# Layer-norm statistics taken in the stage that finishes x, one row tile behind its addition

## The reference, cut to what matters

```python
def _layernorm(x, axis=-1, eps=1e-05):
    m = jnp.mean(x, axis=axis, keepdims=True)
    v = jnp.var(x, axis=axis, keepdims=True)
    return (x - m) / jnp.sqrt(v + eps)
...
    x = x + _L0_gnn_ref(_layernorm(x, axis=-1), edge_index, L0_gnn_weight, L0_gnn_bias)
    x = x + _L0_ffn_ref(_layernorm(x, axis=-1)[None], L0_ffn_Wg, L0_ffn_bg, L0_ffn_We, L0_ffn_be)[0]
```

## Time and profile before

| | |
|---|---|
| time, median of 3 runs | 5624.57 us (5622.45 to 5626.36) |
| the profiled execution's own time | 5618.81 us |
| its span in the profile | 5617.0 us |
| TensorE busy (matmul) | 4898.8 us, 87% |
| TensorE busy (weight load) | 3206.5 us, 57% |
| DVE busy | 2794.0 us, 50% |
| ScalarE busy | 1428.1 us, 25% |
| GpSimd busy | 633.4 us, 11% |

### The profile page before, as it was taken

How to read it: one execution, slowest core, us unless ns; L and a number is a source line. 1 busy time by engine, 2 the same in 40 slices (tenths; PEclk the granted TensorE clock), 3 DMA queues, 4 the chain that set the end, 5 groups by cost and what they waited for, 6 DMA issues and landing times. The chain is left out here.

```text
span 5617.0 us, 281252 instructions
## 1 busy us (share of the span) xinstructions
PE 4898.8 (87%) x116024; PEld 3206.5 (57%) x117274; DVE 2794.0 (50%) x11344; ACT 1428.1 (25%) x4662; POOL 633.4 (11%) x1073
## 2 busy tenths in 40 slices
PE   8899686999898988888888888888888888868789
PEld 6644343444565446666666666666666666644556
DVE  4500344232554665555555555555555555554524
ACT  0000000012232353333333333333333333322313
POOL 0000283000563110000000000000000000010200
PEclk9999897999999999999999999999999999989878
DMA  0000111167443850000000000000000000001000
GB/s 11 15 30 15 28 41 34 45 219 256 137 120 100 296 146 22 12 11 11 11 12 11 11 11 11 12 11 11 11 12 11 11 11 11 8 27 41 16 32 10
DMA packets 153467, 259.51 MB, mean 46 GB/s; under 512 B 47554, under 2 KB 81480, under 8 KB 149037
## 3 DMA queue, kind: packets, MB, share of 16 engines
q1 hardware_dynamic: 98344, 176.13, 9.4%
q0 software_dynamic: 55040, 82.30, 5.1%
HBM read 172.87 MB, written 85.14 MB: 46 GB/s over the span
## 5 line engine op out<-in xcount | busy, mean ns | idle before, releaser
L1558 PE MATMUL bank<-lstm_w,step_h_parts 128*32 128x128 f16 x94848 | 1558.0, 220 | 101.6 <-issue 5.5
L1558 PEld LDWEIGHTS bank<-lstm_w,step_h_parts 128*32 128x32 f16 x94848 | 1341.1, 97 | 451.8 <-issue 300.3
L1630 DVE TRANSPOSE_TENSOR_REDUCE step_summed<-bank 128x4 f32 (+1 forms) x2500 | 792.0, 317 | 1061.1 <-PE bank L1558 895.7
L1553 PE MATMUL bank<-step_xg,step_rows 128*128 (+1 forms) x1252 | 476.0, 381 | 277.9 <-issue 258.2
L1526 ACT ACTIVATE step_act_out<-step_summed,lstm_inv_scale 128x4 f32<-128x4 f32 x625 | 185.8, 297 | 1707.9 <-DVE step_summed L1630 1707.9
L1514 POOL COPY xnT<-step_state 128x4 f32 (+1 forms) x625 | 116.4, 186 | 2743.9 <-DVE step_state L1655 2743.9
L1179 PE MATMUL bank<-sum_parts,sum_hot 125*125 125x512 f16 x1600 | 348.0, 381 | 6.6 <-DVE sum_parts L1138 6.6
L1179 PEld LDWEIGHTS bank<-sum_parts,sum_hot 125*125 125x125 f16 x1600 | 219.8, 137 | 135.2 <-DVE sum_parts L1138 7.7
L1429 PE MATMUL bank<-xg_w,xnT 128*125 128x512 f32 x640 | 277.1, 596 | 6.6 <-DMA xg_w<-in_c_w_ih 6.6
L538 POOL DMA_INDIRECT gcn_rows<-gcn_h_rows,gcn_idx x160 | 202.0, 1262 | 698.6 <-issue 698.3
L1553 PEld LDWEIGHTS bank<-step_xg,step_rows 128*128 128x128 bf16 x2500 | 142.7, 98 | 210.1 <-issue 131.1
(11 more groups left out here) (364 smaller groups left out, 6289.8 us busy)
## 6 DMA issues: line engine op xcount, KB each, us to landing
rel_h<-rel_h_sb SPq DMA_DIRECT2D x39, 1024.0 KB, 6.4
lstm_xg<-cnt POOLq DMA_DIRECT2D x80, 375.0 KB, 4.3
step_xg<-lstm_xg SPq DMA_DIRECT2D x375, 80.0 KB, 2.4
xg_w<-in_c_w_ih SPq DMA_DIRECT2D x16, 1024.0 KB
lstm_w<-in_c_w_hh SPq DMA_DIRECT2D x16, 1024.0 KB, 12.6
cheb_w<-in_L_gnn_weight SPq DMA_DIRECT2D x8, 1024.0 KB
choose_we<-in_L_ffn_experts SPq DMA_DIRECT2D x8, 1024.0 KB
rel_bases<-in_L_gnn_bases SPq DMA_DIRECT2D x8, 1024.0 KB, 11.1
```

Source lines behind the costliest of these rows:

```text
L1553: return nc.tensor.matmul(bank[:], rows[:, p, :], xg[:, at, :], start=True, stop=stop)
L1558: last = nc.tensor.matmul(bank[32 * q:32 * q + 32, 128 * s:128 * s + 128], h_parts[:, c, :], w[:, s, c, q, a, 128 * p:128 * p + 128], star ...
L1630: nc.vector.tensor_reduce(summed[:, 4 * p:4 * p + 4], bank[:, bass.ds(s * 128, 128)].rearrange("p (b r) -> p b r", r=32), X_AXIS, ALU.add, ...
```

## The change: what it does

A semaphore `x_ready` counts finished row tiles of x, five for each layer norm. A new function `take_stats(nc, dve, B, m)` waits for it, takes the `bn_stats` of tile m, and then the `bn_aggr` of tile m - 1. Each stage calls it on DVE: behind the addition of tile m it takes the statistics of tile m - 1, and behind the last addition those of the last tile. For the first layer norm x is the input itself: `x_ready` is raised by five in the constants' block, and edge counting takes the statistics as the first thing on DVE. In `layernorm` only the last tile's `bn_aggr` is left ahead of line 124.

```diff
@@ load_constants
-            nc.vector.memset(B.zero[:], 0.0)
+            nc.vector.memset(B.zero[:], 0.0).then_inc(B.x_ready, NT)
@@ new function
+def take_stats(nc, dve, B, m):
+
+    base = NT * B.ln_calls
+    dve.wait_ge(B.x_ready, base + m + 1)
+    nc.vector.bn_stats(B.stats[:, m, :], B.x[:, m, :]).then_inc(B.ln_stats, 1)
+    if m > 0:
+        dve.wait_ge(B.ln_stats, base + m)
+        nc.vector.bn_aggr(B.mv[:, m - 1, :], B.stats[:, m - 1, :]).then_inc(B.ln_aggr, 1)
@@ layernorm
-            for j in range(NT):
-                nc.vector.bn_stats(B.stats[:, j, :], B.x[:, j, :]).then_inc(B.ln_stats, 1)
-            for j in range(NT):
-                dve.wait_ge(B.ln_stats, base + j + 1)
-                nc.vector.bn_aggr(B.mv[:, j, :], B.stats[:, j, :]).then_inc(B.ln_aggr, 1)
+            dve.wait_ge(B.ln_stats, base + NT)
+            nc.vector.bn_aggr(B.mv[:, NT - 1, :], B.stats[:, NT - 1, :]).then_inc(B.ln_aggr, 1)
             dve.wait_ge(B.ln_aggr, base + NT)
@@ count_edges
         def _(dve):
+            for m in range(NT):
+                take_stats(nc, dve, B, m)
             dve.wait_ge(loaded, 48)
@@ chebyshev
             for m in range(NT):
                 dve.wait_ge(fin, m + 1)
-                nc.vector.tensor_tensor(B.x[:, m, :], B.x[:, m, :], bk[:, 0, m, :], ALU.add).then_inc(fin, 1)
+                nc.vector.tensor_tensor(B.x[:, m, :], B.x[:, m, :], bk[:, 0, m, :], ALU.add).then_inc(B.x_ready, 1)
+                if m > 0:
+                    take_stats(nc, dve, B, m - 1)
+            take_stats(nc, dve, B, NT - 1)
@@ choose_experts
             for e in range(EX):
+                x_step = B.x_ready if e == EX - 1 else added
                 for m in range(NT):
...
-                                                   op0=ALU.mult, op1=ALU.add).then_inc(added, 1)
+                                                   op0=ALU.mult, op1=ALU.add).then_inc(x_step, 1)
+                    if e == EX - 1 and m > 0:
+                        take_stats(nc, dve, B, m - 1)
+            take_stats(nc, dve, B, NT - 1)
@@ add_hidden (LSTM)
                 for c in range(KC):
...
-                    nc.vector.scalar_tensor_tensor(
+                    last = nc.vector.scalar_tensor_tensor(
...
+                last.then_inc(B.x_ready, 1)
+                if m > 0:
+                    take_stats(nc, dve, B, m - 1)
+            take_stats(nc, dve, B, NT - 1)
```

More of the change, by code:

```diff
@@ L62, in allocate @@
     B.bank = [ctx.enter_context(nc.psum_tensor(f"bank{i}", [128, 512], F32)) for i in range(8)]
-    B.ln_stats, B.ln_aggr, B.ln_rstd, B.ln_norm, B.ln_turn, B.ln_xnT, B.ln_var, B.ln_sqrt = [
-        sem(n) for n in ("ln_stats", "ln_aggr", "ln_rstd", "ln_norm", "ln_turn", "ln_xnT", "ln_var", "ln_sqrt")]
+    B.x_ready, B.ln_stats, B.ln_aggr, B.ln_rstd, B.ln_norm, B.ln_turn, B.ln_xnT, B.ln_var, B.ln_sqrt = [
+        sem(n) for n in ("x_ready", "ln_stats", "ln_aggr", "ln_rstd", "ln_norm", "ln_turn", "ln_xnT", "ln_var", "ln_sqrt")]
     B.ln_calls = 0
@@ L448, in _ @@
                 nc.vector.scalar_tensor_tensor(out=B.x[:, m, :], in0=B.bank[m][0:R, :], scalar=gates[:, 0:1],
-                                               in1=B.x[:, m, :], op0=ALU.mult, op1=ALU.add)
+                                               in1=B.x[:, m, :], op0=ALU.mult, op1=ALU.add).then_inc(B.x_ready, 1)
+                if m > 0:
+                    take_stats(nc, dve, B, m - 1)
+            take_stats(nc, dve, B, NT - 1)
         @block.scalar
@@ L589, in _ @@
             for m in range(NT):
-                nc.vector.tensor_tensor(B.x[:, m, :], B.x[:, m, :], B.bank[7][0:R, :], ALU.add)
+                nc.vector.tensor_tensor(B.x[:, m, :], B.x[:, m, :], B.bank[7][0:R, :], ALU.add).then_inc(B.x_ready, 1)
+                if m > 0:
+                    take_stats(nc, dve, B, m - 1)
+            take_stats(nc, dve, B, NT - 1)
         @block.scalar
@@ L1148, in _ @@
                 nc.vector.scalar_tensor_tensor(out=B.x[:, m, :], in0=B.bank[m][0:R, :], scalar=inv, in1=B.x[:, m, :],
-                                               op0=ALU.mult, op1=ALU.add)
+                                               op0=ALU.mult, op1=ALU.add).then_inc(B.x_ready, 1)
+                if m > 0:
+                    take_stats(nc, dve, B, m - 1)
+            take_stats(nc, dve, B, NT - 1)
         @block.scalar
@@ L2088, in _ @@
                 dve.wait_ge(done, m + 1)
-                nc.vector.tensor_tensor(B.x[:, m, :], B.x[:, m, :], B.bank[m][0:R, :], ALU.add)
+                nc.vector.tensor_tensor(B.x[:, m, :], B.x[:, m, :], B.bank[m][0:R, :], ALU.add).then_inc(B.x_ready, 1)
+                if m > 0:
+                    take_stats(nc, dve, B, m - 1)
+            take_stats(nc, dve, B, NT - 1)
 AH = 8
```

## The result

The changed kernel takes 5583.52 us (median of four runs, 5580.44 to 5585.51) where the kernel before, in four runs, takes 5624.39: a ratio of 0.9926 [0.9911, 0.9942], 40.9 us less. The forecast was 5618.3 with a range of 5609 to 5629; it was wrong. Of all the executions in this document two, of the later kernel with two more `bn_stats`, were slow ones (8154.75 and 17526.08 us), and its median is that of the other eight. Two things must be told apart: what the moved statistics did at the eight places between the stages, and what happened in the last stage, which the edit doesn't change.

What follows compares the result with a forecast made beforehand. TensorE, 87% busy, bounds the stages; between them it idles while DVE's layer-norm chain runs. Eight heads gain 23.0 us, stages add 16.7: -6.3, carried to the median 5624.57 as 5618.3 us, range 5609 to 5629.

Steps and rivals of the forecast that it cites:

- TensorE's granted clock falls otherwise: faster: Rival, chance 0.07: the last stage loses its 75 us at 1.2 GHz, kernel at 5585; shifted layer-norm transposes alone, 5613.
- the fall in the last stage comes after a pause there that the edit doesn't touch: Argument against the faster-clock rival: the last stage's drop to half clock, costing 33.5 us, would stay.
- shorter idle ahead of the layer norm's transposes: Argument for the faster-clock rival: TensorE idles less at layer norms, for example 5.8 us after routing instead of 6.85.
- signs of being wrong: Listed: heads keep their length, ScalarE pauses behind its load, DVE gaps before statistics, or last-stage half clock of another length.
- The rival's price: Last stage: 240 matmuls taking 75 us at half clock would need 41.5 at full clock, so 33.5 us.
- The head: Layer norm from first statistic to square root: 0.39 us for 3.65; with a table load, square root 1.29 after its start.
- price for a switch of tables: Skill page's 2.66 us at four heads, each giving back 1.38: whole change -0.8 us, kernel 5623.8.
- The places: Eight layer norms between stages, in order: -2.4, 0, -1.1, 0, -1.9, 0, +0.2, -1.1 us.
- The added waits: DVE waits on `x_ready` and `ln_stats` inside the stages: costed at nothing, +1.8 us if each took 0.04.
- Edge counting: First stage: 3.34 us of moved statistics lie under DVE's 4.0 us wait for loads, so nothing is added.
- The LSTM loop moves: Rival, chance 0.04: each of 625 steps' branches takes 28 ns more, 17.5 us in all, kernel at 5636.
- the sum for the edit: All eight places: 23.0 us gained in the heads, less 16.7 added in the stages, -6.3 us.

Runs made afterwards that it cites:

- later kernel with two more `bn_stats`: Changed kernel plus two unused `bn_stats` at the head of DVE's list in the last stage; 5621.4 us, ratio 0.9992 to the kernel before.
- five more: Kernel before plus five unused `bn_stats` at the head of DVE's list in the last stage; 5592.33 us, ratio 0.9941.
- filled: Kernel before plus four unused TensorE products in the last stage's pause, ahead of the first transposes; 5588.95 us, ratio 0.9936.
- eight more: Kernel before plus eight unused `bn_stats` at the head of DVE's list in the last stage; 5625.76 us, ratio 1.0004.

## Why the prediction was wrong

**The step that failed** is the argument against the rival "TensorE's granted clock falls otherwise: faster", which had 0.07: "the fall in the last stage comes after a pause there that the edit doesn't touch". The premise holds, for the pause is 2.26 us in both traces. The conclusion doesn't follow. The same pause is followed by half clock in three kernels and by full clock in two, with the change and without it; what was moved between them is when it comes, and filling it removes the half clock. In the profiled executions the edit brought the pause's end to 52.00 us behind the clock's last rise from 52.43, and the stage behind it became 36.6 us shorter. The prediction looked for what could change the pause's length, not for what could change its moment, and so it priced the right event (5585, measured 5583.5) and gave it little weight. The price was near, the reason beside it was not: shorter idle ahead of the layer norm's transposes is absent in the kernel before with five more `bn_stats`, where the half clock went away as well. Among its signs of being wrong the prediction had named another length of this half clock, and that sign came.

**The rival's price** was 33.5 us for the stretch of 75 us, and the stage gained 36.6. The first transposes behind the first output projection and the last projection, in the kernel before and in the changed one, show where the rest lies:

```profile
5508.64 0.71 PE L2348 MATMUL bank<-ident,att_p 125*125 125x125 f32 x5
5605.35 6.00 PE L2374 MATMUL bank<-att_wo,att_oT 128*125 128x512 f32 x8 [0.67 <-ACT att_oT L2282]
```

```profile
5471.38 0.71 PE L2380 MATMUL bank<-ident,att_p 125*125 125x125 f32 x5
5567.64 5.39 PE L2406 MATMUL bank<-att_wo,att_oT 128*125 128x512 f32 x8 [0.67 <-ACT att_oT L2314]
```

Behind the pause's end these transposes stand at 78.29 us (5508.64 - 5430.35) and at 42.81 (5471.38 - 5428.57). So the stretch itself cost 35.5, 2.0 more than the price by counts of matmuls; 1.1 more lie at the end of the stage, where the clock fell again, at 5603.2 before and at 5567.7 after.

**The head** went as worked out: the square root stands 0.42 to 0.43 us behind the first `bn_aggr` where no table is loaded (0.39 forecast), 1.29 behind the load's start where one is. The Trainium skill's price for a switch of tables (ScalarE: Activation LUTs, section What ACT_TABLE_LOAD costs) adds a drain of about 1380 ns to the load; none is seen behind the load in any of the four heads: 0.01 us each.

**The places,** heads and tails together, were right to 0.1 us in seven of eight. In Chebyshev 0 was forecast and +0.31 measured: the lone `bn_aggr` starts 1.10 us behind DVE's last instruction, where the first `bn_stats` stood 0.81 behind it before, and the square root comes 0.03 us later than costed; the row of additions and statistics itself went as costed (575.03 + 0.17 - 568.85 = 6.35 us, forecast 3.09 + 3.25). Why the barrier takes 0.29 us longer there stays open. The added waits cost nothing that shows: statistics stand behind their additions at DVE's own step.

**Edge counting** covered its statistics, as said: the casts start 0.54 us behind DVE's last aggregate, when `w` has landed.

**"The LSTM loop moves"** didn't happen in a way that can be told: kernels that are the same up to the last stage reach its layer norm's square root at 5352.34 (before), 5358.85 (five more), 5358.69 (filled) and 5358.04 us (eight more). That spread of 6.5 us, between executions of the same instructions, is larger than the whole direct effect. It is also why the two first traces mislead: at the last square root the changed kernel is only 2.5 us ahead (5349.86), because the profiled execution of the kernel before was a short one, 5.6 us under the median of 5624.39.

So the sum for the edit was right within 0.6 us (-6.3 and -5.74), and the forecast was off by 35 because of an event that the sum doesn't hold.

**What stays open:** why the moment decides, and why it is so steady. Executions of one kernel differ by up to 9 us (5618.55 to 5627.20 in 15 runs) and yet, by the mean granted clock, all of them fall or none does. The runs show that the rise and the pause shift together, not what ties them. The Trainium skill (TensorE: Matmul & The Clock Gate, section Part 1: The HAM clock gate) says that the chip's monitor runs freely and doesn't restart with a kernel, so that one kernel's runs differ in where the clock changes; by that, kernels so near the limit would be expected to show both outcomes among their runs, and none of them does.

## What to carry to other kernels

Where a trace shows a long stretch at half clock behind a short pause, an edit upstream can switch it on or off, as the change and the extra `bn_stats` did here: price it as a lottery of that size in every forecast, in both directions, and don't count a kernel's gain as the edit's before the pause has been filled in both versions. Filling it was a repair by itself: four unused products in a wait of 2.26 us gave 36.2 us here and made the time indifferent to a shift that otherwise cost 38. And measure an edit of a few microseconds from an untouched event to the next fixed one, which repeats to 0.02 us, not by end times that scatter by 9.

## What the runs showed of the hardware

- A pause of 2.26 us on TensorE, behind some 50 us of products at 2.4 GHz, was followed by 75.1 us at 1.2 GHz in three kernels and by none in two, though the work behind it is the same 19 records per tile. Where the clock fell, it fell 1.52 to 2.18 us after the pause had ended, with TensorE at work. An attention tile took 5.82 us at half clock, 3.08 at full.
- A kernel became 32.8 us faster by five more instructions on DVE that nobody uses.
- DVE's first instruction behind a layer norm's barrier starts 0.77 to 1.23 us behind its last one ahead of it in the changed kernel, and 0.75 to 1.59 in the kernel before: the 0.81 of the earlier trace rows is one place's number.
